# First pass of a fused attention and router block: transposing the normalised rows by 16 small transfers and VectorE instead of by TensorE

## The chip, the cores and the metric

The kernel runs on one core of a Trainium2 chip. The metric is the device time of one launch in microseconds (us), the median of several runs. Engines are named PE (TensorE matmul), PEld (its weight load), DVE (VectorE), ACT (ScalarE), POOL (GpSimd) and SP (SyncE, which issues every DMA here).

## What is computed

The input is 8192 rows of 512 numbers. A row is normalised, modulated, sent through a linear attention of 16 heads (sums over all rows come first, then each row is used again), added back, normalised again and sent through a router with eight small experts. The reference, cut to what matters here:

```python
h = _layernorm(x) * (1 + ca) + sa
q = elu(h @ Wq.T + bq) + 1 ;  k = elu(h @ Wk.T + bk) + 1 ;  v = h @ Wv.T + bv     # 16 heads of 32
KV = einsum('bhsd,bhsm->bhmd', k, v)
Z = 1 / (einsum('bhsd,bhd->bhs', q, k.sum(axis=2)) + 1e-6)
x = x + ga * (einsum('bshd,bhmd,bhs->bshm', q, KV, Z) @ Wo.T + bo)
h = _layernorm(x) * (1 + cb) + sb
x = x + gb * ffn(h)            # value projection, router with top 2 of 8, experts of 32 hidden units
```

## The kernel before

The rows are worked in 64 tiles of 128 rows. The **first pass** (to about 627 us) needs, for each tile, the normalised rows `xn` and their transpose `xT`; the second pass works in pairs of tiles and is not touched. Every engine runs its own list of instructions and the lists meet only at semaphores. Each engine has a function `step(i, s)`, called for i = -2 or -1 to 64; tile 20 to tile 59 are in a hardware loop of two steps a turn (`sweep`, `LOOP_A`), the rest is written out.

Products are taken at high precision by splitting each operand into a high part and a rest (`_hi`, `_lo`) and adding three products (function `three`, lines 1394, 1395 and 1399). One tile in step i goes as follows.

- PE: four 128x128 transposes of `xn(i+1)` into one PSUM bank, `bank_xT` (L1507); `k(i)` = 12 matmuls of `xT(i)` with `wk`; the sum M over rows of `k(i-1)` with `xn(i-1)`, 12 matmuls; `q(i)`, 12 matmuls with `wq`.
- ACT: the high part of `xT(i+1)` (L720), relu and exp for `q(i-1)` (L724, L726) and `k(i)` (L731, L733), the high parts of `k` (L737) and `xn` (L742).
- DVE: `zq(i-1)` (L1107), `xT_lo(i+1)` (L888), statistics of tile i+2 (L867), `qf(i-1)` (L1116), `zk(i)` (L1123), `xn(i+2)` (L882, after POOL has the reciprocal root, L593), `kf(i)` (L1132), `k_lo(i)` (L1138), then the next step's `zq`.
- SP: the load of tile i+4 (L538), special loads of step i (`loads`), the store of `q(i-1)` to DRAM (L543).

Steps 0 to 19 also carry the preparation of all weights, in a table `PREP` that gives each step up to three jobs; they put extra instructions on PE, ACT and DVE (for instance `modulation`, L990 and L993, and for six jobs `scaled`, L1014, which stands between `kf` and `k_lo`). The `loads` of step 2 fetch `Wo` in 16 transfers of short pieces (L500, `raw_o`).

Of the kernel before, what the change touches and what calls it, by code (L numbers as in the profile page):

```python
# [48 lines left out]
PREP = {0: ["", "", "bk", "bq"], 3: ["v0", "v1"], 4: ["v2", "v3"], 5: ["bv", ""], 6: ["", "ga"], 7: ["o0", "o1"],  # L49
# [17 lines left out]
def sweep(eng, step, first, last, loop_from, loop_to):  # L67

    for i in range(first, loop_from):
        step(i, i % 2)  # L70
    with eng.Fori(loop_from, loop_to, 2) as v:
        step(v, 0)
        step(v + 1, 1)
    for i in range(loop_to + 1, last + 1):
        step(i, i % 2)
# [28 lines left out]

def build(nc, x, Wq, bq, Wk, bk, Wv, bv, Wo, bo, fWv, fbv, Wg, bg, Wp, alpha, g_r, b_r, g_c, b_c,
# [3 lines left out]
    LOOP_A = (PREP_STEPS, T - 5)  # L109
# [9 lines left out]
    with ctx:  # L119
# [21 lines left out]
        ca1_col = sb("ca1_col", [P, KB])  # L141
        ks_acc = sb("ks_acc", [P, D])
# [171 lines left out]
        xT_psum = sem("xT_psum")  # L314
# [16 lines left out]
        q_out = [sem("q_out0"), sem("q_out1")]  # L331

# [123 lines left out]
        def _(sp):  # L456
# [88 lines left out]
            sweep(sp, step, -2, T, *LOOP_A)  # L545

# [22 lines left out]
        def _(pool):  # L569
# [35 lines left out]
            sweep(pool, step, -2, T - 1, *LOOP_A)  # L605
# [64 lines left out]
        def _(act):  # L670
# [36 lines left out]

            act.wait_ge(prep_taken, TAKE["sa"] + 1)
            for b in range(KB):
                hi_scaled(f"k{b}", wk_hi[:, b, :], ca1_col[:, b:b + 1])  # L710
            for b in range(KB):
                hi_scaled(f"q{b}", wq_hi[:, b, :], ca1_col[:, b:b + 1])


            def step(i, s):
                if live(i + 1, T):
                    act.wait_ge(xT_psum, i + 2)
                    wait_count(act, xTl_done, i)
                    wait_count(act, q_psum, i)
                    nc.scalar.copy(xT_hi[:, 1 - s, :], bank_xT).then_inc(xTh_done, 1)  # L720
# [7 lines left out]
                if live(i, T):  # L728
# [4 lines left out]
                    nc.scalar.activation(exp_k[:, s, :], exp_k[:, s, :], ACT.Exp, scale=-1.0).then_inc(ek_done, 1)  # L733
                    act.wait_ge(kf_done, i + 1)
# [10 lines left out]
            sweep(act, step, -1, T, *LOOP_A)  # L745
# [105 lines left out]
        def _(dve):  # L851
# [25 lines left out]
            def normed(i, s):  # L877
                dve.wait_ge(rstd_done, i + 1)
                wait_count(dve, xT_psum, i - 1)
# [3 lines left out]
                                        ALU.subtract, ALU.mult).then_inc(xn_done, 1)  # L883

# [48 lines left out]
            nc.vector.tensor_copy(sa_col[:], bank("sa")[:, 0:KB])  # L933
            taken_by(nc.vector.tensor_scalar(ca1_col[:], bank("sa")[:, KB:2 * KB], 1.0, None, ALU.add), "sa")
# [89 lines left out]
            def prepare(i, n):  # L1024

                for j in prep_job(i, n):
# [76 lines left out]
            def step(i, s):  # L1103
# [4 lines left out]
                if live(i + 1, T):  # L1108
                    xT_low(i + 1, 1 - s)
# [10 lines left out]
                if live(i, T):  # L1120
                    dve.wait_ge(k_psum, i + 1)
                    wait_count(dve, ek_done, i - 1)
                    nc.vector.tensor_tensor(zk[:, s, :], bank_k, bk_row[:], ALU.add).then_inc(zk_done, 1)  # L1123
                prepare(i, 0)
                if ahead:
                    var_eps(i + 2, s)
                    normed(i + 2, s)
                if live(i, T):
                    dve.wait_ge(ek_done, i + 1)
                    wait_count(dve, kh_done, i - 1)  # L1130
                    wait_count(dve, ks_done, i - 1)
# [17 lines left out]
            sweep(dve, step, 0, T, *LOOP_A)  # L1149
# [236 lines left out]
        def _(pe):  # L1386
# [23 lines left out]

            def blocks_of(raw, fb):
# [264 lines left out]
```

## Time and profile before

| | |
|---|---|
| median of 3 runs | 1314.85 us (1313.02 to 1316.6) |
| profiled execution | 1313.38 us, its span 1311.7 us |
| busy share of the span | PE 96%, PEld 79%, DVE 74%, ACT 41%, POOL 43% |
| mean granted TensorE clock | 0.991 |
| `zq` of tile 0, of tile 19, and of tile 63 on DVE | 38.1 us, 243.4 us, 626.8 us |

The span is from the first to the last instruction; the 1.7 us beside it lie outside. A matmul's end is modelled, so how far apart the starts of two matmuls lie says more than their durations.

### The profile page before, as it was taken

Reading aid. Unit: us, or ns where it says so; the run is one execution under the profiler, and the core shown is the slowest. Engines: PE = TensorE matmul, PEld = TensorE weight load, DVE = VectorE, ACT = ScalarE, POOL = GpSimd, SP = SyncE. Lnnn points to the kernel's source line nnn. Section 1 sums busy time; section 2 is a strip of 40 time slices with the busy share of each in tenths; the row PEclk is TensorE's granted clock in tenths of the full one; section 3 lists DMA queues with packets and bytes.
Section 4 is the critical chain, followed back from the end, with each engine's and each line's share of the span. In section 5 each row is a group of like instructions: output and inputs, shape, how many; then the busy total and the mean of one; then the engine's idle time right before and its main releaser. Section 6 shows DMA issues by size and latency. Waiting matters only on the chain.

```text
span 1311.7 us, 19601 instructions
## 1 busy us (share of the span) xinstructions
PE 1255.9 (96%) x6078; PEld 1034.4 (79%) x6078; DVE 973.8 (74%) x2195; ACT 541.7 (41%) x1125; POOL 557.9 (43%) x397
## 2 busy tenths in 40 slices
PE   7999999999999999999779999999999999999998
PEld 7777877788888888888568888878888888888887
DVE  7778887866666666665767778777778788787764
ACT  2443544454444444444234344343343343433431
POOL 1332333344344334433346455455464454554631
PEclk8999999999999999999899999999999999999999
DMA  6643211111122111111312231231321322312201
GB/s 208 161 150 88 65 49 49 49 64 64 48 63 64 61 51 64 64 51 47 104 49 77 69 97 60 86 97 49 98 82 63 97 67 79 97 57 89 81 17 49
DMA packets 93467, 99.12 MB, mean 76 GB/s; under 512 B 21720, under 2 KB 54616, under 8 KB 93392
## 3 DMA queue, kind: packets, MB, share of 16 engines
q1 hardware_dynamic: 93392, 98.21, 24.1%
q8 instruction: 37, 0.61, 0.2%
q14 instruction: 38, 0.31, 0.1%
HBM read 64.63 MB, written 33.55 MB: 75 GB/s over the span
## 4 chain that ended last, share of the span: by engine, by line
PE 56%; POOL 15%; issue 13%; DVE 7%; ACT 2%; DMA 0%; POOLq 0%; SPq 0%; ACTq 0%; DVEq 0%
PE ps L1395 17%; PE ps L1394 17%; PE ps L1399 17%; POOL xb L610 6%; POOL rrs L649 3%; PE ps L1593 2%; POOL xn_lo L602 2%; POOL rstd L642 2%; DVE x L1222 2%; DVE xT_lo L1229 1%; PE ps L1507 1%; POOL ks_acc L598 1%; DVE marked L1312 1%; ACT xn L806 1%; POOL rstd L593 1%
## 5 line engine op out<-in xcount | busy, mean ns | idle before, releaser
L636 POOL TENSOR_TENSOR cn<-c,half 128x16 f32<-128x16 f32 x32 | 104.2, 3255 | 281.5 <-DVE c L1257 281.5
L593 POOL TENSOR_TENSOR rstd<-veps,neg_half 128x1 f32<-128x1 f32 x64 | 35.2, 550 | 286.3 <-DVE veps L875 286.3
L598 POOL TENSOR_TENSOR ks_acc<-ks_acc,kf 128x512 f32<-128x512 f32 x64 | 82.9, 1295 | 102.7 <-DVE kf L1132 102.7
L602 POOL TENSOR_TENSOR xn_lo<-xn,xn_hi 128x512 fp32r<-128x512 f32 x64 | 110.9, 1733 | 7.4 <-ACT xn_hi L742 7.4
L1394 PE MATMUL ps<-g_hi,qT_hi 128*128 128x512 f32 x256 | 104.6, 409 | 4.9 <-ACT qT_hi L770 4.9
L1138 DVE TENSOR_TENSOR k_lo<-kf,k_hi 128x512 fp32r<-128x512 f32 x64 | 75.4, 1178 | 43.8 <-ACT k_hi L737 36.5
L1394 PE MATMUL ps<-wk_hi,xT_hi 128*128 128x512 f32 x256 | 106.2, 415 | 0.0
L1394 PE MATMUL ps<-k_hi,xn_hi 128*128 128x512 f32 x256 | 102.7, 401 | 1.4 <-DVE bq_row L1051 1.4
L1394 PE MATMUL ps<-wq_hi,xT_hi 128*128 128x512 f32 x256 | 103.7, 405 | 0.0
L1394 PE MATMUL ps<-v_hi,xT_hi 128*128 128x512 f32 x256 | 102.6, 401 | 0.0
L1395 PE MATMUL ps<-g_lo,qT_hi 128*128 128x512 f32 x256 | 101.9, 398 | 0.0
L1395 PE MATMUL ps<-wq_lo,xT_hi 128*128 128x512 f32 x256 | 101.3, 396 | 0.0
L1395 PE MATMUL ps<-wk_lo,xT_hi 128*128 128x512 f32 x256 | 101.3, 396 | 0.0
L1399 PE MATMUL ps<-k_hi,xn_lo 128*128 128x512 f32 x256 | 101.2, 395 | 0.0
L1395 PE MATMUL ps<-k_lo,xn_hi 128*128 128x512 f32 x256 | 101.1, 395 | 0.0
L1395 PE MATMUL ps<-v_lo,xT_hi 128*128 128x512 f32 x256 | 100.0, 391 | 0.0
L763 ACT CAST xT_hi<-ps 128x512 fp32r<-128x512 f32 x64 | 37.5, 587 | 132.3 <-PE ps L1593 132.3
L731 ACT ACTIVATE exp_k<-zk 128x512 f32<-128x512 f32 x64 | 40.4, 632 | 110.7 <-DVE zk L1123 110.7
L628 POOL TENSOR_TENSOR qks<-q_in,ks_q 128x1024 f32<-128x1024 f32 x32 | 77.1, 2409 | 14.9 <-DMA q_in<-q_scratch 8.3
L1394 PE MATMUL ps<-c_hi,xT_hi 128*128 128x328 f32 x256 | 80.7, 324 | 0.0
L610 POOL TENSOR_TENSOR xb<-xin,bo_ga 128x1024 f32<-128x1024 f32 x32 | 78.3, 2446 | 1.7 <-PE ps L1399 1.6
L720 ACT CAST xT_hi<-ps 128x512 fp32r<-128x512 f32 x64 | 37.5, 586 | 98.6 <-PE ps L1507 98.6
(241 smaller groups left out, 3358.3 us busy)
## 6 DMA issues: line engine op xcount, KB each, us to landing
xin<-_attn_hidden_states_dram SPq DMA_DIRECT2D x64, 256.0 KB, 2.8
q_scratch<-qf SPq DMA_DIRECT2D x64, 256.0 KB, 2.9
xin<-_attn_hidden_states_dram SPq DMA_DIRECT2D x32, 512.0 KB, 4.1
q_in<-q_scratch SPq DMA_DIRECT2D x128, 128.0 KB, 2.9
out_dram<-qf SPq DMA_DIRECT2D x64, 256.0 KB, 2.1
wm_in<-in_L_wmod_dram SPq DMA_DIRECT2D x4, 1024.0 KB, 6.9
wm_in<-in_L_wmod_dram SPq DMA_DIRECT2D x4, 512.0 KB, 6.7
raw_k<-in_L_attn_Wk_dram SPq DMA_DIRECT2D x1, 1024.0 KB, 10.1
```

The costliest lines, as they stand in the source:

```text
L593: nc.gpsimd.tensor_tensor(rstd[:, s:s + 1], veps[:, s:s + 1], neg_half[:, 0:1], ALU.pow).then_inc(rstd_done, 1)
L598: nc.gpsimd.tensor_tensor(ks_acc[:], ks_acc[:], kf[:, s, :], ALU.add).then_inc(ks_done, 1)
L602: nc.gpsimd.tensor_tensor(xn_lo[:, 1 - s, :], xn[:, 1 - s, :], f32(xn_hi[:, 1 - s, :]), ALU.subtract).then_inc(xnl_done, 1)
L610: nc.gpsimd.tensor_tensor(xb[:], xin[:], bo_ga[:].unsqueeze(1).to_broadcast([P, 2, D]), ALU.add).then_inc(xb_done, 1)
L628: nc.gpsimd.tensor_tensor(qks[:].rearrange("p h (g f) -> p (h g) f", f=P), q_of(j).rearrange("p (n f) -> p n f", f=P), ks_q[:].unsqueeze(1 ...
L636: nc.gpsimd.tensor_tensor(cn[:].rearrange("p h e -> p (h e)"), c2[:].rearrange("p h e -> p (h e)"), half[:], ALU.pow).then_inc(cn_done, 1)
L649: nc.gpsimd.tensor_tensor(rrs[:].rearrange("p h k -> p (h k)"), rve[:], neg_half[:, 0:4], ALU.pow).then_inc(rrs_done, 1)
L731: nc.scalar.activation(exp_k[:, s, :], zk[:, s, :], ACT.Relu, scale=-1.0).then_inc(rk_done, 1)
L1138: nc.vector.tensor_tensor(k_lo[:, s, :], kf[:, s, :], f32(k_hi[:, s, :]), ALU.subtract).then_inc(kl_done, 1)
L1394: nc.tensor.matmul(dst, ah, bh, start=start and n == 0, stop=False)
L1395: nc.tensor.matmul(dst, ah, bl, start=False, stop=False)
L1399: last = nc.tensor.matmul(dst, al_, bh, start=False, stop=stop and n == len(parts) - 1)
```

## The change

`xn` of a tile is no longer transposed on PE (apart from tiles 0 and 1). Instead SP issues 16 SBUF-to-SBUF transfers, each 32 partitions by 128 numbers, which move the blocks of `xn` into a new buffer `xq`; DVE then transposes `xq` in blocks of 32x32 straight into `bank_xT` (`turned_x`). To make that possible the blocks of `xT` hold every fourth column instead of 128 neighbours, so `wk` and `wq` and their scales are prepared for that order (`every_fourth`, `sa4_col`, `ca4_col`), and the scales in the old order are made by a new preparation job `sc` in step 1. The read of `xq` steps over four numbers for each one that it takes (`f` is outside `j` in memory).

On ACT the high part of `xT` moves from the start of the step to between exp and `k_hi`; on DVE `xT_lo` moves from behind `zq` to between `kf` and `k_lo`. `kf` is now written over `zk`. On SP the step's special loads come last. All first-pass steps are written out; the hardware loop is gone. The diff, cut:

```diff
-PREP = {0: ["", "", "bk", "bq"], 3: ["v0", "v1"], 4: ["v2", "v3"], 5: ["bv", ""], 6: ["", "ga"], 7: ["o0", "o1"],
+PREP = {0: ["", "", "bk", "bq"], 1: ["sc"], 3: ["v0", "v1"], 4: ["v2", "v3"], 5: ["bv", ""], 6: ["", "ga"], 7: ["o0", "o1"],
...
+def sweep_tiles(step, first, last):
+
+    for i in range(first, last + 1):
         step(i, i % 2)
...
+        xq = sb("xq", [P, 2, D], F32, early)
         exp_k = sb("exp_k", [P, 2, D], F32, early)
-        kf = sb("kf", [P, 2, D], F32, early)
+        kf = zk
...
             def step(i, s):
+                if live(i + 2, T) and i >= 0:
+                    sp.wait_ge(xn_done, i + 3)
+                    sp.wait_ge(xTb_done, i + 1)
+                    for g in range(KB):
+                        for c4 in range(KB):
+                            sp.dma_start(xq[DH * c4:DH * (c4 + 1), s, g * P:(g + 1) * P],
+                                         xn[DH * g:DH * (g + 1), s, c4 * P:(c4 + 1) * P]).then_inc(xq_in[s], 16)
                 if live(i + 4, T):
...
+            def turned_x(i, s):
+                dve.wait_ge(xq_in[s], regrouped(i, s))
+                dve.wait_ge(xTl_done, i)
+                nc.vector.transpose(bank_xT.rearrange("p (j g t) -> p g j t", j=KB, g=KB),
+                                    xq[:, s, :].rearrange("p (g f j) -> p g j f", g=KB, j=KB)).then_inc(xTb_done, 1)
...
+            def every_fourth(raw, fb):
+                return [raw[:, r, fb::KB] for r in range(KB)]
...
             pe.wait_ge(wk_in, 16)
             for b in range(KB):
-                transposes(f"k{b}", blocks_of(raw_k, b))
+                transposes(f"k{b}", every_fourth(raw_k, b))
...
             def step(i, s):
-                if live(i + 1, T):
+                if isinstance(i, int) and i <= 0:
                     pe.wait_ge(xn_done, i + 2)
...
                     for b in range(KB):
-                        blk = slice(b * P, (b + 1) * P)
-                        last = nc.tensor.transpose(bank_xT[:, blk], xn[:, 1 - s, blk], ident[:])
-                    last.then_inc(xT_psum, 1)
+                        last = nc.tensor.transpose(bank_xT[:, b * P:(b + 1) * P], xn[:, 1 - s, b::KB], ident[:])
+                    last.then_inc(xTb_done, 1)
```

DVE's list in step 2, before the change, from `zq` to the `k_lo` of the same step:

```order
L1107 TENSOR_TENSOR zq<-ps,bq_row 128x512 [waits eq_done,q_psum]
L888 TENSOR_TENSOR xT_lo<-ps,xT_hi 128x512 [waits q_psum,xTh_done]
L867 BN_STATS stats<-xin 128x6 [waits x_in0]
L1116 SCALAR_TENSOR_TENSOR qf<-zq,exp_q 128x512 [waits eq_done,stats_done]
L871 BN_AGGR mv<-stats 128x2
L1123 TENSOR_TENSOR zk<-ps,bk_row 128x512 [waits ek_done,k_psum]
L875 TENSOR_SCALAR veps<-mv 128x1 [waits mv_done]
L882 TENSOR_SCALAR xn<-xin,mv,rstd 128x512 [waits xnh_done,xnl_done,xT_psum,rstd_done]
L1132 SCALAR_TENSOR_TENSOR kf<-zk,exp_k 128x512 [waits ks_done,kh_done,ek_done]
L1138 TENSOR_TENSOR k_lo<-kf,k_hi 128x512 [waits m_done,kh_done,kf_done]
```

The same step after the change (`kf` bears the name `zk`, over which it is written):

```order
L1134 TENSOR_TENSOR zq<-ps,bq_row 128x512 [waits q_psum]
L882 BN_STATS stats<-xin 128x6 [waits x_in0]
L1144 SCALAR_TENSOR_TENSOR qf<-zq,exp_q 128x512 [waits eq_done,stats_done]
L886 BN_AGGR mv<-stats 128x2
L1152 TENSOR_TENSOR zk<-ps,bk_row 128x512 [waits ks_done,kh_done,k_psum]
L890 TENSOR_SCALAR veps<-mv 128x1 [waits mv_done]
L900 TENSOR_SCALAR xn<-xin,mv,rstd 128x512 [waits xnh_done,xnl_done,xq_in0,rstd_done]
L906 STREAM_TRANSPOSE ps<-xq 128x4x4x32 [waits xTl_done,xq_in1]
L1161 SCALAR_TENSOR_TENSOR zk<-zk,exp_k 128x512 [waits ek_done]
L912 TENSOR_TENSOR xT_lo<-ps,xT_hi 128x512 [waits q_psum,xTh_done]
L1169 TENSOR_TENSOR k_lo<-zk,k_hi 128x512 [waits m_done,kh_done,kf_done]
```

One 128x512 transpose is new, behind `xn`, and waits for the 16 transfers of the tile before (`xq_in1`); `xT_lo` stands between `kf` and `k_lo`.

SP's list from step 1's special loads to step 2's, before:

```order
L495 DMA bv_row<-in_L_attn_bv_dram 128x4x32 x4
L543 DMA q_scratch<-qf 128x512 [waits qf_done]
L538 DMA xin<-in_L_attn_hidden_states_dram 128x512 [waits xn_done]
L500 DMA raw_o<-in_L_attn_Wo_dram 128x4x32 x16
L543 DMA q_scratch<-qf 128x512 [waits qf_done]
```

And after, down to the transfers of step 3:

```order
L498 DMA bv_row<-in_L_attn_bv_dram 128x4x32 x4
L544 DMA xq<-xn 32x128 [waits xTb_done,xn_done]
L544 DMA xq<-xn 32x128 x15
L548 DMA xin<-in_L_attn_hidden_states_dram 128x512 [waits xn_done]
L551 DMA q_scratch<-qf 128x512 [waits qf_done]
L503 DMA raw_o<-in_L_attn_Wo_dram 128x4x32 x16
L544 DMA xq<-xn 32x128 [waits xTb_done,xn_done]
L544 DMA xq<-xn 32x128 x15
```

Each step's 16 transfers now stand behind the special loads of the step before, in one queue.

## Rows read from the trace of the kernel before

**Rows 1.** Windows: us, busy of each engine (instructions), clock, DMA share, GB/s.

```profile
150.00:250.00 100.00, 96.89 (x442) 76.54 (x441) 82.73 (x145) 44.50 (x78) 32.65 (x28) 1.00 0.16 49
262.00:590.00 328.00, 328.00 (x1491) 266.18 (x1491) 220.67 (x375) 155.87 (x263) 132.24 (x113) 1.00 0.19 59
```

**Rows 2.** Timeline of PE: start us, duration us, what, idle before.

```profile
407.27 0.48 PE L1394 MATMUL ps<-wk_hi,xT_hi 128*128 128x512 f32 x1
...
416.07 0.48 PE L1394 MATMUL ps<-wk_hi,xT_hi 128*128 128x512 f32 x1
...
618.27 0.39 PE L1394 MATMUL ps<-wk_hi,xT_hi 128*128 128x512 f32 x1
...
626.63 0.40 PE L1394 MATMUL ps<-k_hi,xn_hi 128*128 128x512 f32 x1
```

**Rows 3.** Timeline of DVE in the loop.

```profile
407.11 0.69 DVE L1107 TENSOR_TENSOR zq<-ps,bq_row 128x512 f32<-128x512 f32 x1 [0.74 <-PE ps L1399]
```

**Rows 4.** Timeline of DVE, the ends of the preparation and its waits.

```profile
38.11 0.69 DVE L1107 TENSOR_TENSOR zq<-ps,bq_row 128x512 f32<-128x512 f32 x1
...
89.59 0.69 DVE L1107 TENSOR_TENSOR zq<-ps,bq_row 128x512 f32<-128x512 f32 x1 [1.56 <-PE ps L1399]
...
196.41 0.69 DVE L1107 TENSOR_TENSOR zq<-ps,bq_row 128x512 f32<-128x512 f32 x1 [1.10 <-PE ps L1399]
...
202.52 0.56 DVE L943 SCALAR_TENSOR_TENSOR c_lo<-ps,cb_col,c_hi 128x328 fp32r<-128x328 f32 x1 [2.18 <-ACT c_hi L677]
...
243.37 0.69 DVE L1107 TENSOR_TENSOR zq<-ps,bq_row 128x512 f32<-128x512 f32 x1
```

**Rows 5.** Timeline of DVE, one written-out step (step 18).

```profile
220.58 0.69 DVE L1107 TENSOR_TENSOR zq<-ps,bq_row 128x512 f32<-128x512 f32 x1
...
222.69 0.69 DVE L1116 SCALAR_TENSOR_TENSOR qf<-zq,exp_q 128x512 f32<-128x512 f32 x1 [0.22 <-DVE stats L867]
...
223.39 0.66 DVE L1123 TENSOR_TENSOR zk<-ps,bk_row 128x512 f32<-128x512 f32 x1
...
224.77 0.55 DVE L882 TENSOR_SCALAR xn<-xin,mv,rstd 128x512 f32<-128x512 f32 x1 [0.66 <-POOL rstd L593]
225.41 0.69 DVE L1132 SCALAR_TENSOR_TENSOR kf<-zk,exp_k 128x512 f32<-128x512 f32 x1
226.84 1.18 DVE L1138 TENSOR_TENSOR k_lo<-kf,k_hi 128x512 fp32r<-128x512 f32 x1 [0.74 <-ACT k_hi L737]
227.95 0.68 DVE L1075 TENSOR_TENSOR b2raw<-ps,b2raw 128x512 f32<-128x512 f32 x1
```

**Rows 6.** Groups of DVE instructions, each shape apart: busy us, mean ns | idle before.

```profile
L1239 DVE STREAM_TRANSPOSE qTf<-qz 128x1024 f32<-128x1024 f32 x32 | 39.6, 1238 | 0.1
...
L1211 DVE TENSOR_TENSOR qz<-q_in,zr 128x1024 f32<-128x1024 f32 x32 | 39.2, 1226 | 1.1
...
L1020 DVE TENSOR_TENSOR v_lo<-wtmp,v_hi 128x512 fp32r<-128x512 f32 x4 | 7.1, 1776 | 0.0
```

**Rows 7.** Timeline of DVE, a step with `scaled` (step 12).

```profile
161.25 0.75 DVE L1014 SCALAR_TENSOR_TENSOR wtmp<-ps,cb_col,mod 128x512 f32<-128x512 f32 x1
162.07 1.18 DVE L1138 TENSOR_TENSOR k_lo<-kf,k_hi 128x512 fp32r<-128x512 f32 x1
```

**Rows 8.** Timeline of SP's DMA issues: start us, time to issue all.

```profile
45.02 5.01 SPq L495 DMA_DIRECT2D bv_row<-in_L_attn_bv_dram  x4
...
52.95 10.65 SPq L500 DMA_DIRECT2D raw_o<-in_L_attn_Wo_dram  x16
...
123.76 1.99 SPq L520 DMA_DIRECT2D b2raw<-in_L_ffn_b_dram  x6
...
645.65 1.79 SPq L531 DMA_DIRECT2D q_in<-q_scratch  x4
```

**Rows 9.** DMA issues: KB each, median us from issue to landing.

```profile
out_dram<-qf SPq DMA_DIRECT2D x64, 256.0 KB, 2.1
```

**Rows 10.** Timeline of PEld, the first weight transposes.

```profile
15.03 3.46 PEld L1407 LDWEIGHTS ps<-ident,raw_k 128*128 128x128 f32 x16
```

More of the change, by code:

```diff
@@ L64, in wait_count @@
         eng.wait_ge(sem, n)
[L67 to L74, printed above, removed]
+def sweep_tiles(step, first, last):
+    for i in range(first, last + 1):
         step(i, i % 2)
@@ L543, in step @@
                     sp.dma_start(q_dram[rows(i - 1), :], qf[:, 1 - s, :]).then_inc(q_out[1 - s], 16)
-            sweep(sp, step, -2, T, *LOOP_A)
+                if isinstance(i, int):
+                    loads(i)
+            sweep_tiles(step, -2, T)
             sp.wait_ge(q_out[0], landed(T - 2, 0))
@@ L733, in step @@
                     nc.scalar.activation(exp_k[:, s, :], exp_k[:, s, :], ACT.Exp, scale=-1.0).then_inc(ek_done, 1)
+                    if live(i + 1, T) and i > 0:
+                        xT_high(i, s)
                     act.wait_ge(kf_done, i + 1)
@@ L743, in step @@
                 prepare(i, 1)
-            sweep(act, step, -1, T, *LOOP_A)
+            sweep_tiles(step, -1, T)
             act.wait_ge(m_done, T)
@@ L878, in normed @@
                 dve.wait_ge(rstd_done, i + 1)
-                wait_count(dve, xT_psum, i - 1)
+                if isinstance(i, int) and i <= 3:
+                    wait_count(dve, xTb_done, i - 1)
+                else:
+                    dve.wait_ge(xq_in[s], regrouped(i - 2, s))
                 wait_count(dve, xnh_done, i - 1)
@@ L1127, in step @@
                     normed(i + 2, s)
+                if live(i + 1, T) and not early_turn:
+                    turned_x(i + 1, 1 - s)
                 if live(i, T):
                     dve.wait_ge(ek_done, i + 1)
-                    wait_count(dve, kh_done, i - 1)
-                    wait_count(dve, ks_done, i - 1)
                     nc.vector.scalar_tensor_tensor(out=kf[:, s, :], in0=zk[:, s, :], scalar=0.0,
@@ L1134, in step @@
                     scaled(i)
+                    if live(i + 1, T) and not early_turn:
+                        xT_low(i + 1, 1 - s)
                     dve.wait_ge(kf_done, i + 1)
@@ L1147, in step @@
                     router_constants()
-            sweep(dve, step, 0, T, *LOOP_A)
+            sweep_tiles(step, 0, T)
             dve.wait_ge(m_done, T)
@@ L1433, in _, with strided_columns @@
             all_rows, first_row = ones[:, 0:1], ident[:, 0:1]
+            def strided_columns(j, col, part):
+                for b in range(KB):
+                    last = nc.tensor.matmul(bank(j)[:, col + b:col + b + 1], part[:, b::KB], all_rows, start=True, stop=True)
+                return last
             pe.wait_ge(mod1_done, KB)
-            columns("sa", 0, [(mod1[:, 0, :], all_rows)])
-            columns("sa", KB, [(mod1[:, 1, :], all_rows)]).then_inc(prep_psum, 1)
+            strided_columns("sa", 0, mod1[:, 0, :])
+            strided_columns("sa", KB, mod1[:, 1, :]).then_inc(prep_psum, 1)
             pe.wait_ge(wk_in, 16)
             for b in range(KB):
-                transposes(f"k{b}", blocks_of(raw_k, b))
+                transposes(f"k{b}", every_fourth(raw_k, b))
             pe.wait_ge(wq_in, 16)
             for b in range(KB):
-                transposes(f"q{b}", blocks_of(raw_q, b))
+                transposes(f"q{b}", every_fourth(raw_q, b))
             SUMS = {"ga": 0, "gb": 3}
@@ L1454, in prepare @@
                         sum_rows(j, acc_q[:])
+                    elif j == "sc":
+                        bank_free(pe, j)
+                        columns(j, 0, [(mod1[:, 0, :], all_rows)])
+                        columns(j, KB, [(mod1[:, 1, :], all_rows)]).then_inc(prep_psum, 1)
                     elif j in SUMS:
@@ L1540, in step @@
                 prepare(i, 2)
-            sweep(pe, step, -1, T, *LOOP_A)
+            sweep_tiles(step, -1, T)
             pe.wait_ge(ks_done, T)
```

51 lines of the change are left out of this document (30 added, 21 removed).

## The prediction

> **What bounds the kernel now.** I read the windows first. In the loop (262 to 590 us) PE is busy in all of 328 us, and DVE in 221; in the preparation DVE's share is higher, 83 of 100 us [rows 1]. So the first pass has two regimes, and I asked of each which wait ends last.
>
> In the loop it is PE. One tile takes 416.07 - 407.27 = 8.80 us, and DVE's first instruction of the step waits 0.74 us for PE's last matmul [rows 2, 3]. The trace also holds one tile without the four transposes, at the end of the pass: from 618.27 to 626.63 PE does the same 36 matmuls in 8.36 us, 0.232 each [rows 2]. The transposes therefore cost **0.44 us a tile**: their own time and the slower first matmul behind them (0.48 against 0.39 us).
>
> In the preparation it is DVE. Its `zq` starts at 38.11 us for tile 0 and at 243.37 for tile 19: 19 steps of 10.8 us on average, and in all of them only three waits that come from PE, 1.56 and 1.10 us directly and 2.18 through ACT [rows 4]. What PE saves in these steps is worth nearly nothing, and what DVE gets in addition is paid in full, unless it falls into a hole of DVE's own.
>
> **PE's part.** From step 22 on, after two steps in which DVE catches up, to step 62 there are 41 steps: 41 x 0.44 = **-18.0 us**. In the two stretches of the preparation that PE sets (ended by the waits of 1.56 and of 1.10 with 2.18) it saves one transposition each, **-0.9**.
>
> **DVE's step.** The written-out step 18 gives its length without PE [rows 5]: `zq` to `qf` 2.11, set by relu and exp on ACT, since DVE idles 0.22 ahead of `qf`; `qf` to `zk` 0.70; `zk` to `xn` 1.38, with 0.66 of waiting for POOL; `xn` 0.47; `kf` to `k_lo` 1.43, with 0.74 of waiting for ACT's `k_hi`; `k_lo` 1.11. Sum 7.20. (An instruction frees DVE some 0.08 before its listed end: `k_lo` is listed with 1.18 and the next starts after 1.11.) `xT_lo`, 0.61, leaves a place where ACT sets the pace and goes into the 0.74 hole: nothing gained and nothing lost. Its cover is gone in six steps, where `scaled` fills that hole already: there `k_lo` starts 0.82 after a `scaled` of 0.75 [rows 7], room for 0.15 to 0.18, so 0.43 each, **+2.6**. ACT's copy of the high part runs beside `kf`, ahead of `k_hi`, and is no longer than `kf`.
>
> **The new transpose.** The nearest row is `turned_q`: 1.24 us for 1024 numbers a partition, the same as a plain two-input operation of that size, 1.23 [rows 6]. At that rate 512 numbers take 0.69 (like `qf` in rows 5), which occupies 0.61. But `turned_q` reads runs of 32 neighbours, while `turned_x` reads one number in four, each 16 bytes from the last. No row here shows such a read. I bound it by 0.69 below and by the whole 1.24 above, twice the time for a number, and take the upper end, **1.24, occupying 1.16**, because nothing of the neighbour that a read brings along can be used. The slowest 512-number row of DVE, 1.78 [rows 6], bounds it for the rival.
>
> The Trainium skill (Vector Engine (DVE) Microarchitecture Reference, Measured stream behaviour on trn2) speaks against the change here: a port keeps its full rate only while it reads at least two adjacent 4-byte words at a time; a source that hops every element took 1.73 ns a column against 1.05, and 2.5 with small steps. By those figures an estimate for this transpose is 1.0 to 1.4 us, and my sum would be 5 us lower or 9 higher.
>
> The transpose stands in steps 1 to 19 of the preparation. In two of them the waits for PE absorb it, so 17 x 1.16 = **+19.7 us**. In the later steps DVE's step becomes 7.20 + 1.16 = 8.36, exactly PE's 8.36. Two engines with no room between them lose a little; I take 8.40, 41 x 0.04 = **+1.6**.
>
> **The transfers.** SP's 16 issues follow the end of `xn(i+2)`; the transpose of that tile follows the end of `xn(i+3)`, one step later. Issue: six short transfers took 1.99 us, 0.33 each, four of 128 KB 1.79, 0.45 each [rows 8]. A transfer of 32 short rows is nearer to the former: 16 x 0.34 = 5.4. Landing: 2.1 us is the shortest of the large ones [rows 9]. With 0.2 for SP to notice, the transpose can start 0.2 + 5.4 + 2.1 = 7.7 us after `xn`, and a step has 8.4: hidden, with 0.7 to spare. If they are late by more, the order lets DVE run on in between: two steps must hold one DVE step and one transfer time X, so the step is (8.36 + X)/2 and nothing is lost up to X = 8.4. SP itself needs 5.4 + 0.7 for the load and the store, of 8.4. The load of tile i+4 and the store are now 5.4 later, but are needed more than a step later.
>
> In the preparation the special loads are ahead of the next transfers in the queue. Steps 1 and 2 are the heavy ones. A step there is 10.8 + 1.0 = 11.8 long with the new transpose. Step 1: 5.4 + 0.9 + 5.0 for `bv_row` [rows 8] + about 1.7 for three large loads = 13.0: 1.2 late. Step 2: 5.4 + 0.7 + 10.65 of `raw_o` [rows 8] = 16.8, and step 3's transfers need 7.5 more: 1.2 + 24.3 against two steps of 11.8, a stall of **+1.9** in step 4. Behind it stand `kf`, `k_lo` and so PE's M. Nothing at all or 8 us, if the pieces of `raw_o` drain slowly, are the ends. The other loads fit.
>
> **Small parts.** Job `sc`: two short DVE operations and a wait, **+0.5**; its eight PE columns lie where PE waits for DVE. The 32 weight transposes read every fourth column; 16 weight loads took 3.46 us [rows 10], between nothing and double for these, mostly beside DVE's work, **+1.0**. The loop's disappearance: the written-out steps show the same 0.232 between matmuls; nothing.
>
> **Sum.** -18.0 - 0.9 + 2.6 + 19.7 + 1.6 + 1.9 + 0.5 + 1.0 = **+8.4 us** on the profiled execution's 1313.4, 1321.8. The median of the runs shown lies 1.5 higher, within their spread; I predict 1322. A measurement here tells a difference of about 0.3% (3.9 us) from none.
>
> **Rivals.**
> 1. *The strided read costs nothing extra* (0.69). For it: the transpose reshuffles anyway and `turned_q` shows no price over a plain operation [rows 6]; against it the stride above. 17 x 0.61 = 10.4 in place of 19.7, and no 1.6: -2.5, 1311. This is the side that isn't slower. The balance is at a duration of 0.84 us. If the stall and the start-up term also fail to appear it is -5.4, 1308. Chance 0.26.
> 2. *The transfers are late in every step.* If 16 issues take 0.45 each, as for `q_in`, X = 7.2 + 2.1 + 0.2 = 9.5 and the step (8.36 + 9.5)/2 = 8.93: 41 x 0.53 = 22 more, 1344. At `raw_o`'s 0.67 each SP alone needs 11.3 a step, and the pass would be 120 us longer. Against it: the pieces are few and long compared with those. Chance 0.13.
> 3. *DVE becomes the bound*: a transpose over 1.24. At 1.43 the step is 8.55: 3.2 more in the preparation and 41 x 0.15 = 6.2, 1331; at 1.78 it is 1352. By the Trainium skill's figure for small steps (same page and section) this is the case that comes. Chance 0.15.
> 4. Something in the start-up or the catching up that I don't see, either way: 0.04.
>
> The forecast has 0.42; alone it spans 1315 to 1329. **Range** 1309 to 1340: it leaves out rival 1 with both favours, and the far ends of 2 and 3. Faster by over 0.3%: 0.10 from rival 1, 0.03 from the forecast's edge, 0.03 others, **0.16**. Within 0.3%: 0.14 and 0.08, **0.22**. Slower: **0.62**.
>
> **What would show it.** In the profile after: the transpose's mean duration (0.69 or 1.24); the distance between PE's `wk_hi` groups in the later tiles (8.36 to 8.40; 8.5 or more would be DVE or the transfers, told apart by whether DVE waits for `xq` ahead of the transpose); DVE's `zq` of tile 19 at some 243.4 + 25 = 268 us, and no wait for PE left there beyond two; one wait for `xq` of about 2 us near 80 us; SP's issue time of 16 transfers, 5.4; the second pass of unchanged length. I am wrong if the transpose is cheap, if transfers issue at over 0.4 us each, or if DVE's holes, into which I put `xT_lo`, close.

## The result, and the profile after

The changed kernel takes **1480.86 us** (median, 1479.95 to 1484.14) against 1315.32 (1313.02 to 1316.6) before: 1.1275 times as long, interval 1.1256 to 1.1295. The forecast was 1322, range 1309 to 1340.

The page of the changed kernel: busy time of PE and DVE, the clock, the chain that ended last, and three groups and an issue row.

```profile
PE 1288.9 (87%) x5846; PEld 1041.6 (70%) x5846; DVE 1025.2 (69%) x2259; ACT 545.7 (37%) x1125; POOL 558.2 (38%) x397
...
PEclk9969899989999999999999899999999999999999
...
SPq 31%; PE 24%; issue 20%; POOL 14%; DVE 7%; ACT 2%; DMA 1%; POOLq 0%; ACTq 0%; DVEq 0%
SPq L544 28%; PE ps L1425 7%; PE ps L1426 7%; PE ps L1430 7%; POOL xb L620 5%; POOL rrs L659 3%; POOL xn_lo L612 2%; PE ps L1636 2%; POOL ks_acc L608 2%; SPq L548 2%; POOL rstd L652 1%; DVE x L1253 1%; DVE xT_lo L1260 1%; SPq L551 1%; POOL rstd L603 1%
...
L1425 PE MATMUL ps<-wk_hi,xT_hi 128*128 128x512 f32 x256 | 123.3, 481 | 135.7 <-ACT xT_hi L722 133.7
...
L906 DVE STREAM_TRANSPOSE ps<-xq 128x512 f32<-128x512 f32 x62 | 67.9, 1096 | 170.7 <-DMA xq<-xn 170.6
...
xq<-xn SPq DMA_DIRECT2D x992, 16.0 KB, 1.8
```

The chain is where to begin: 28% of the span hangs on SP's queue at L544, the line that issues the new transfers. Not on DMA (1%), whose transfers land 1.8 us after their issue, and not on DVE. DVE waited 170.6 us for `xq`, PE 133.7 us for ACT's `xT_hi`, which stands behind DVE's transpose: the same stall, seen one and two engines further on.

The windows of [rows 1], after the change:

```profile
150.00:250.00 100.00, 82.64 (x343) 63.46 (x342) 75.51 (x128) 37.61 (x65) 27.79 (x23) 0.93 0.27 71
262.00:590.00 328.00, 266.77 (x1044) 205.79 (x1042) 201.96 (x337) 121.98 (x203) 99.81 (x85) 0.94 0.25 69
```

PE does 1044 matmuls in 328 us, where it did 1491 (four of 40 a tile being transposes). No compute engine is full any more. Which one is shows in the timeline of SP (start us, time to issue all):

```profile
497.69 10.02 SPq L544 DMA_DIRECT2D xq<-xn  x16
507.76 0.58 SPq L548 DMA_DIRECT2D xin<-_attn_hidden_states_dram  x1
508.38 0.43 SPq L551 DMA_DIRECT2D q_scratch<-qf  x1
508.91 10.40 SPq L544 DMA_DIRECT2D xq<-xn  x16
519.36 0.58 SPq L548 DMA_DIRECT2D xin<-_attn_hidden_states_dram  x1
519.98 0.43 SPq L551 DMA_DIRECT2D q_scratch<-qf  x1
520.51 10.02 SPq L544 DMA_DIRECT2D xq<-xn  x16
```

SP has no gap: 16 issues, the load, the store, the next 16. A round is 11.22 and then 11.60 us, and 0.63 to 0.65 us of it goes to each of the 16. Over all tiles behind the 20th a round averages 11.5 us; in about half of the rounds the 16 issues take longer than 10.0, up to 11.2, and the trace doesn't say why. The pass runs at SP's pace. DVE's timeline in the same place, the ends of one step:

```profile
501.25 0.68 DVE L1134 TENSOR_TENSOR zq<-ps,bq_row 128x512 f32<-128x512 f32 x1
...
505.56 0.55 DVE L900 TENSOR_SCALAR xn<-xin,mv,rstd 128x512 f32<-128x512 f32 x1 [0.66 <-POOL rstd L603]
508.94 1.09 DVE L906 STREAM_TRANSPOSE ps<-xq 128x512 f32<-128x512 f32 x1 [2.83 <-DMA xq<-xn]
...
510.69 0.69 DVE L912 TENSOR_TENSOR xT_lo<-ps,xT_hi 128x512 fp32r<-128x512 f32 x1
511.36 1.18 DVE L1169 TENSOR_TENSOR k_lo<-zk,k_hi 128x512 fp32r<-128x512 f32 x1
512.46 0.68 DVE L1134 TENSOR_TENSOR zq<-ps,bq_row 128x512 f32<-128x512 f32 x1
```

The wait for `xq` (2.83 us) is the only long one; `k_lo` follows `xT_lo`, and `zq` follows `k_lo`, without a hole. The row names DMA, since the last landing releases it; but the last issue of that tile only ended at 507.7 (first row of SP above), 1.2 us before DVE starts. The issue was late, not the landing.

Three rows of DVE split the time: `zq` of tiles 0, 19 and 63, as in [rows 4] and, for the last, 626.83 in the kernel before.

```profile
38.08 0.69 DVE L1134 TENSOR_TENSOR zq<-ps,bq_row 128x512 f32<-128x512 f32 x1
...
297.21 0.69 DVE L1134 TENSOR_TENSOR zq<-ps,bq_row 128x512 f32<-128x512 f32 x1
...
794.41 0.68 DVE L1134 TENSOR_TENSOR zq<-ps,bq_row 128x512 f32<-128x512 f32 x1
```

The same differences for every kernel of this study, in us, read off these rows of each. They are used throughout below; the last column is the span less the `zq` of tile 63, which is the end of the first pass and the whole second.

| kernel | first `zq` | tile 0 to 19 | tile 19 to 63 | rest of the span |
|---|---|---|---|---|
| before | 38.11 | 205.26 | 383.46 | 684.87 |
| after | 38.08 | 259.13 | 497.20 | 687.69 |
| no_transfers | 39.43 | 221.87 | 366.48 | 685.72 |
| no_transfers_contig | 39.69 | 213.56 | 366.11 | 687.64 |
| eight_wide | 38.19 | 225.48 | 366.49 | 685.84 |
| from_dram | 38.17 | 234.52 | 386.20 | 686.01 |
| two_queues | 38.02 | 237.54 | 367.35 | 687.19 |
| bounce | 39.34 | 221.63 | 366.49 | 684.84 |
| bounce_late | 38.79 | 206.01 | 366.48 | 684.72 |

Of the 170.4 us that the span grew, 53.9 lie in the preparation, 113.7 in the tiles behind it, 2.8 after. The start is as it was. The 113.7 are a mean over unlike tiles: 497.20 / 44 is 11.30, less than a round of SP, since the last tiles have no transfers to wait for (tile 62 to 63 takes 7.24).

### The profile page after: what moved, and what is told of

Same layout as the page of the kernel before. It is cut to its first block, busy times and chain, and to the rows that moved or that the text cites. A ratio compares the mean times of both kernels' runs of the same rounds, so it can differ in the third digit from the quotient of the medians.

```text
span 1482.1 us, 19445 instructions
## 1 busy us (share of the span) xinstructions
PE 1288.9 (87%) x5846; PEld 1041.6 (70%) x5846; DVE 1025.2 (69%) x2259; ACT 545.7 (37%) x1125; POOL 558.2 (38%) x397
## 4 chain that ended last, share of the span: by engine, by line
SPq 31%; PE 24%; issue 20%; POOL 14%; DVE 7%; ACT 2%; DMA 1%; POOLq 0%; ACTq 0%; DVEq 0%
SPq L544 28%; PE ps L1425 7%; PE ps L1426 7%; PE ps L1430 7%; POOL xb L620 5%; POOL rrs L659 3%; POOL xn_lo L612 2%; PE ps L1636 2%; POOL ks_acc L608 2%; SPq L548 2%; POOL rstd L652 1%; DVE x L1253 1%; DVE xT_lo L1260 1%; SPq L551 1%; POOL rstd L603 1%
## 5 line engine op out<-in xcount | busy, mean ns | idle before, releaser
L1425 PE MATMUL ps<-wk_hi,xT_hi 128*128 128x512 f32 x256 | 123.3, 481 | 135.7 <-ACT xT_hi L722 133.7
L608 POOL TENSOR_TENSOR ks_acc<-ks_acc,zk 128x512 f32<-128x512 f32 x64 | 82.7, 1293 | 324.7 <-DVE zk L1161 324.7
L906 DVE STREAM_TRANSPOSE ps<-xq 128x512 f32<-128x512 f32 x62 | 67.9, 1096 | 170.7 <-DMA xq<-xn 170.6
L1425 PEld LDWEIGHTS ps<-wk_hi,xT_hi 128*128 128x128 f32 x256 | 56.3, 220 | 171.9 <-ACT xT_hi L722 157.9
L1426 PE MATMUL ps<-wk_lo,xT_hi 128*128 128x512 f32 x256 | 117.5, 459 | 0.0
L737 ACT ACTIVATE exp_q<-zq 128x512 f32<-128x512 f32 x64 | 40.4, 632 | 135.5 <-DVE zq L1134 135.5
L1144 DVE SCALAR_TENSOR_TENSOR qf<-zq,exp_q 128x512 f32<-128x512 f32 x64 | 44.3, 693 | 54.0 <-DVE stats L882 48.3
```

The costliest lines, as they stand in the source:

```text
L608: nc.gpsimd.tensor_tensor(ks_acc[:], ks_acc[:], kf[:, s, :], ALU.add).then_inc(ks_done, 1)
L906: nc.vector.transpose(bank_xT.rearrange("p (j g t) -> p g j t", j=KB, g=KB), xq[:, s, :].rearrange("p (g f j) -> p g j f", g=KB, j=KB)).th ...
L1144: nc.vector.scalar_tensor_tensor(out=qf[:, 1 - s, :], in0=zq[:, 1 - s, :], scalar=0.0, in1=exp_q[:, 1 - s, :], op0=ALU.max, op1=ALU.add).t ...
L1425: nc.tensor.matmul(dst, ah, bh, start=start and n == 0, stop=False)
L1426: nc.tensor.matmul(dst, ah, bl, start=False, stop=False)
```

## The experiments

The theory: one engine's time for issuing is the bound, because an SBUF-to-SBUF transfer costs SyncE about 0.6 us to issue whatever its size, and there are sixteen a tile. The rivals: the landing or the DMA engines are too slow; the turn on VectorE, the stride or the written-out steps cost the time; the price goes by bytes or by rows.

**probe_issues.** The price by itself, after the kernel before has ended. One of the groups, the others alike:

```diff
             sp.wait_ge(stored[1], landed(T - 1, 1))
+            for g in range(KB):
+                for c4 in range(KB):
+                    sp.dma_start(xin[DH * c4:DH * (c4 + 1), 0, g * P:(g + 1) * P],
+                                 xn[DH * g:DH * (g + 1), 0, c4 * P:(c4 + 1) * P]).then_inc(probe, 16)
+            done[0] += 16
+            sp.wait_ge(probe, 16 * done[0])
```

> The kernel before, with transfers added behind its last store, in groups that SyncE issues one after the other, each group waited for before the next; each group has a line of its own. They overwrite no output. Groups: 16 of the change's shape (32 partitions by 128 elements, SBUF to SBUF, across partitions), 16 of it within the same partitions, 16 from DRAM, 16 to DRAM, 16 of 8 partitions by 128, 16 of 8 by 512, 16 of one row of 128, 8 of 128 by 128 SBUF to SBUF, 8 of 128 by 128 from DRAM, 8 of 32 by 256, 2 whole tiles in, 2 out, and 4 of the change's shape alone, each waited for. Theory 'SBUF at both ends': the first two groups cost SyncE 0.60 to 0.65 us a transfer with nothing else running, those with DRAM at one end 0.33 to 0.45. Rival 'rows': the price follows the partitions of the transfer, so 8 partitions and one row cost clearly less than 32 (0.35 against 0.65) and 128 more. Rival 'any transfer': all cost 0.6 or more, one row too. Rival 'full queue': the four single ones cost 0.35 and only long rows of issues 0.65.

Timeline of SP behind the last store. In this order: the change's shape, the same within partitions, from DRAM, to DRAM, 8 partitions by 128, 8 by 512, one row, 128 by 128 in SBUF, the same from DRAM, 32 by 256, and the single ones (in their row the time holds three of the waits).

```profile
1314.95 10.12 SPq L570 DMA_DIRECT2D xin<-xn  x16
1326.29 10.00 SPq L575 DMA_DIRECT2D xin<-xn  x16
1337.52 7.32 SPq L580 DMA_DIRECT2D xin<-q_scratch  x16
1346.05 7.28 SPq L585 DMA_DIRECT2D q_scratch<-xn  x16
1354.42 11.11 SPq L589 DMA_DIRECT2D xin<-xn  x16
1366.64 10.63 SPq L593 DMA_DIRECT2D xin<-xn  x16
1378.64 10.04 SPq L597 DMA_DIRECT2D xin<-xn  x16
1389.82 5.07 SPq L601 DMA_DIRECT2D xin<-xn  x8
1396.25 3.70 SPq L605 DMA_DIRECT2D xin<-q_scratch  x8
1401.43 5.00 SPq L610 DMA_DIRECT2D xin<-xn  x8
...
1413.80 5.72 SPq L622 DMA_DIRECT2D xin<-xn  x4
```

With SBUF at both ends a transfer costs 0.63 us from issue to issue (10.12 / 16), with DRAM at either end 0.46 (7.32 / 16). Bytes and rows hardly matter among these shapes, all of which move pieces of 512 bytes or more: one row of 128 elements 0.63, 128 by 128 elements 0.63, 8 by 128 even 0.69. Short pieces are another case, which the probe leaves out: `raw_o` (512 pieces of 128 bytes each) comes from DRAM and costs 0.67, `bv_row` 1.25 [rows 8]. The trace's own duration of one is 0.591 us for the change's shape, 0.421 from DRAM, and 0.510 for the single ones, each waited for. So a little, 0.08 of 0.59, comes from issuing in a row; most is there with nothing ahead. "SBUF at both ends" holds, with the other kind just above the upper end of what I had put (0.45). "Rows", "any transfer" and "full queue" fall. What inside the issue takes the 0.17 more isn't visible in a trace.

**no_transfers.** Is that all, or does something else in the change cost time?

```diff
-                    sp.wait_ge(xTb_done, i + 1)
-                    for g in range(KB):
-                        for c4 in range(KB):
-                            sp.dma_start(xq[DH * c4:DH * (c4 + 1), s, g * P:(g + 1) * P],
-                                         xn[DH * g:DH * (g + 1), s, c4 * P:(c4 + 1) * P]).then_inc(xq_in[s], 16)
...
+            link(nc.vector.memset(xq[:], 0.0))
...
-                dve.wait_ge(xq_in[s], regrouped(i, s))
```

(SP's wait `xTb_done` and the wait for the transfers in `normed` go too. DVE now transposes zeros.)

> The changed kernel without its sixteen transfers a tile; VectorE transposes a buffer that was set to zero once, so the first pass works on zeros there (the output is not the reference's). Everything else of the change stays: the turn on VectorE, the strided weights, the written-out steps. Theory 'SyncE's issues bound the first pass': all of the 166 us goes with them and the time is 1300 to 1325 us, near the sum of the forecast's other terms (1322). Rival 'the turn itself or the written-out code costs': 1400 or more stays. Rival 'VectorE's access to every fourth element slows its neighbours': 1340 to 1380.

1314.34 us (1312.3 to 1318.94), ratio to before 1.0003, interval 0.9992 to 1.0015. All of the loss goes with the transfers. The long window:

```profile
262.00:590.00 328.00, 327.18 (x1409) 263.96 (x1408) 262.78 (x434) 167.48 (x276) 138.91 (x118) 1.00 0.21 63
```

PE is full again and the clock at its full 2.4 GHz. The table has what the change does without its transfers: +16.6 us in the preparation, -17.0 behind it. The steady tile takes 8.367 us (mean of the 20 from tile 40 to 60), as forecast from the one tile without transposes [rows 2]. The two signs cancel, and the rivals on the turn, the stride's effect on neighbours and the written-out code fall.

**eight_wide.** Price by the transfer or by the byte?

```diff
-                        for c4 in range(KB):
-                            sp.dma_start(xq[DH * c4:DH * (c4 + 1), s, g * P:(g + 1) * P],
-                                         xn[DH * g:DH * (g + 1), s, c4 * P:(c4 + 1) * P]).then_inc(xq_in[s], 16)
+                        for h in range(2):
+                            sp.dma_start(xq[DH * (3 - g):DH * (4 - g), s, h * 2 * P:(h + 1) * 2 * P],
+                                         xn[DH * g:DH * (g + 1), s, h * 2 * P:(h + 1) * 2 * P]).then_inc(xq_in[s], 16)
```

> The changed kernel with 8 transfers of 32 partitions by 256 elements a tile in place of 16 of 32 by 128: the same bytes, the same rows to each transfer, half the number of transfers; the elements land in other places, so the output is not the reference's. Theory 'a price for each transfer': 8 x 0.65 + 1.2 = 6.4 us of SyncE in a step of 8.4, nothing late, 1310 to 1330 us. Rival 'by bytes': each costs 1.3, SyncE needs 11.6 again, 1480. Rival 'landing or engines of the queue': the last transfer's landing of 1.8 us sets VectorE's start whatever the number, and 1380 or more stays.

1317.85 us (1316.83 to 1319.69), ratio 1.003, interval 1.002 to 1.004. The same bytes in half the transfers lose nothing in the steady tiles: 366.49 us from tile 19 to 63, like no transfers at all. By the transfer, then, among transfers with pieces of 512 bytes or more. Its SP timeline:

```profile
450.89 4.95 SPq L544 DMA_DIRECT2D xq<-xn  x8
455.88 1.18 SPq L548 DMA_DIRECT2D xin<-_attn_hidden_states_dram  x1
457.11 0.43 SPq L551 DMA_DIRECT2D q_scratch<-qf  x1
459.25 4.95 SPq L544 DMA_DIRECT2D xq<-xn  x8
```

0.62 each and 1.7 us free in the round. What it loses is one wait in the preparation, 4.98 us, at the transpose behind `raw_o`'s sixteen issues (DVE's timeline):

```profile
81.63 1.09 DVE L906 STREAM_TRANSPOSE ps<-xq 128x512 f32<-128x512 f32 x1 [4.98 <-DMA xq<-xn]
```

**from_dram.** The same sixteen with the cheaper kind of source.

```diff
-                                         xn[DH * g:DH * (g + 1), s, c4 * P:(c4 + 1) * P]).then_inc(xq_in[s], 16)
+                                         xt[rows(i + 2), :][DH * g:DH * (g + 1), c4 * P:(c4 + 1) * P]).then_inc(xq_in[s], 16)
```

> The changed kernel with the same sixteen destinations a tile, 32 partitions by 128 elements, but read from the input in DRAM in place of the normalized tile in SBUF; the first pass so works on x not normalized (the output is not the reference's). Theory 'SBUF at both ends costs': an issue falls to 0.33 to 0.45 us as the loads with DRAM at one end, 16 x 0.4 + 1.2 = 7.6 us a step, 1310 to 1335 us. Rival 'a price for each transfer of this shape, wherever it comes from': 0.65 again and 1470 to 1485 us.

1348.01 us (1346.43 to 1349.93), ratio 1.0255, interval 1.0238 to 1.0272. The theory was right in direction and its upper end 13 us short. SP's timeline:

```profile
445.59 7.38 SPq L544 DMA_DIRECT2D xq<-_attn_hidden_states_dram  x16
453.02 0.42 SPq L548 DMA_DIRECT2D xin<-_attn_hidden_states_dram  x1
453.49 0.43 SPq L551 DMA_DIRECT2D q_scratch<-qf  x1
454.09 7.40 SPq L544 DMA_DIRECT2D xq<-_attn_hidden_states_dram  x16
```

At 0.46 a transfer a round of SP is 8.5 us, already more than PE's 8.37, and SP still has no gap: 0.1 to 0.2 us between the store and the next transfers, where eight_wide has 1.7. As in the changed kernel, some groups of 16 take longer, 7.3 to over 8 us, and a round averages 8.8. So SP's issuing alone nearly gives the tile. The prediction's formula for a late chain gives almost the same: 7.4 of issues, 1.7 of landing (this kernel's median) and 0.2 are 9.3, and (8.2 + 9.3) / 2 = 8.75; the table has 386.20 / 44 = 8.78. This run doesn't tell the two apart. My expectation had neither the formula nor a price above 0.45.

**two_queues.** If one engine's issue time is short, a second engine's should do.

```diff
-                    for g in range(KB):
-                        for c4 in range(KB):
+                    for n in range(10):
+                        g, c4 = n // KB, n % KB
...
+            def pair(n0, s):
+                for n in (n0, n0 + 1):
+                    g, c4 = n // KB, n % KB
+                    nc.scalar.dma_start(xq[DH * c4:DH * (c4 + 1), s, g * P:(g + 1) * P],
+                                        xn[DH * g:DH * (g + 1), s, c4 * P:(c4 + 1) * P]).then_inc(xq_in[s], 16)
```

(`pair(10, s)` ahead of `xT_high`, `pair(12, s)` behind `xn_hi`, `pair(14, 1 - s)` in the next step ahead of relu.)

> The changed kernel with the same sixteen SBUF-to-SBUF transfers a tile, ten issued by SyncE and six by ScalarE, two in each of the three gaps that ScalarE has in a step (0.99, 1.56 and 1.50 us in the kernel without transfers). The result is that of the reference. Theory 'what is short is one engine's issue time': at 0.65 each SyncE needs 10 x 0.65 + 1.2 = 7.7 us, the chain behind xn 6.5 + 1.8 + 0.2 = 8.5 us, and ScalarE's pairs of 1.3 us nearly fit their gaps; the later steps go from 11.3 back to 8.4 to 8.6 and the time to 1315 to 1330 us. Rival 'SBUF-to-SBUF transfers as such are slow, or the issues of two engines share one generator': the step stays at 10 us or more, 1400 and over. Rival 'ScalarE pays': its step is 4.3 + 6 x 0.65 = 8.2 with waits, exp and the high parts come late, 9 to 9.5 us a step, 1345 to 1370.

1331.51 us (1330.48 to 1335.35), ratio 1.0143, interval 1.0117 to 1.0168; the expectation ended at 1330. The steady tiles are whole again: 367.35 us, 0.9 above no transfers. The same sixteen transfers land in time when two engines issue them, so the DMA engines' work on them wasn't the limit, and the rival of a shared generator falls. A second engine brings a queue of its own, so this run alone doesn't part the engine's time from its queue's; the probe's single transfers, 0.51 us each with nothing ahead of them, speak for the engine's. ACT's timeline, its queue's issues (ACTq) among its instructions:

```profile
485.61 0.63 ACT L745 ACTIVATE exp_q<-exp_q 128x512 f32<-128x512 f32 x1
485.62 1.25 ACTq L721 DMA_DIRECT2D xq<-xn  x2
487.72 0.63 ACT L752 ACTIVATE exp_k<-zk 128x512 f32<-128x512 f32 x1 [1.48 <-DVE zk L1166]
```

This pair starts with the instruction ahead of it and is done when `zk` comes; `exp_k` doesn't wait for it. The Trainium skill (DMA: Bandwidth & Descriptors, Issuing engines are not separate DMA queues) says that transfers started by different engines share the same 16 DMA engines, and that a second engine saves only the time to initiate them, which is "usually small relative to the DMA itself". That the two share them no run here shows; the mean busy share of the 16 in the later tiles is 0.25 in the changed kernel and 0.34 here, far from full. The second part doesn't hold here: sixteen issues take 10 us and a landing 1.8. What remains over the kernel without transfers lies nearly all in the preparation (237.54 us against 221.87): DVE's waits for `xq` there add up to 14.8 us, in steps where SyncE's special loads stand in the same queue.

**bounce.** Fewer issues for the same regrouping: one store to DRAM and four gathering loads.

```diff
-                    sp.wait_ge(xTb_done, i + 1)
-                    for g in range(KB):
...
+                    sp.dma_start(x_dram[rows(i + 2), :], xn[:, s, :]).then_inc(x_out[s], 16)
...
+                if live(i + 2, T) and i >= 0:
+                    sp.wait_ge(xTb_done, i + 1)
+                    sp.wait_ge(x_out[s], landed(i, s))
+                    for c4 in range(KB):
+                        sp.dma_start(xq[DH * c4:DH * (c4 + 1), s, :].rearrange("p (g f) -> p g f", f=P),
+                                     x_dram[rows(i + 2), c4 * P:(c4 + 1) * P].rearrange("(g i) f -> i g f", i=DH)
+                                     ).then_inc(xq_in[s], 16)
```

> The changed kernel with the regrouping taken through DRAM: one store of the normalized tile, a wait for it on SyncE, then four loads that gather the rows, 5 issues with DRAM at one end in place of 16 with SBUF at both. The result is that of the reference. Theory 'the count times the price of an issue': 5 x 0.42 + 0.9 = 3 us of SyncE; the chain of store, landing, four issues and landing is 0.4 + 2.5 + 1.8 + 2.5 = 7.2 us, under the 8.4 of a step, so nothing waits and the time is that of the kernel without transfers, 1312 to 1322 us. Rival 'latency, not issue, is the trouble': two landings one behind the other are over 8.4 us and VectorE waits for them as before, 1340 or more. Rival 'SyncE, blocked in the wait for the store, holds up its other work in the preparation': a stall or two near 80 us, 1320 to 1330.

1315.77 us (1313.68 to 1316.6), ratio 1.0009, interval 1.0 to 1.0019: level with no transfers at all. SP's timeline:

```profile
439.81 0.34 SPq L543 DMA_DIRECT2D x_scratch<-xn  x1
440.19 0.43 SPq L546 DMA_DIRECT2D xin<-_attn_hidden_states_dram  x1
440.67 0.44 SPq L549 DMA_DIRECT2D q_scratch<-qf  x1
441.90 1.78 SPq L554 DMA_DIRECT2D xq<-x_scratch  x4
```

3 us of issuing a tile. The detour moves more: the DMA engines' busy share in the long window is 0.41, where it was 0.19 before the change [rows 1], and DVE never waits for `xq`. The loads start 2.1 us after the store and are issued at 443.7; with the 2.4 us of their landing the chain is 6.3 us, under a step. Two landings, one behind the other, cost nothing here, and neither does SP's wait in the preparation (221.63 us to tile 19, 221.87 without transfers).

**no_transfers_contig.** What is the stride worth?

```diff
-                                    xq[:, s, :].rearrange("p (g f j) -> p g j f", g=KB, j=KB)).then_inc(xTb_done, 1)
+                                    xq[:, s, :].rearrange("p (g j f) -> p g j f", g=KB, j=KB)).then_inc(xTb_done, 1)
```

> The kernel without transfers, and VectorE's transpose reads neighbouring elements in place of every fourth (it works on zeros, so the output is not the reference's). Theory 'the stride is what makes the transpose 1.10 us': 0.69 us each, 17 x 0.41 = 7 us less in the preparation, nothing in the steps that TensorE sets: 1304 to 1310 us. Rival 'the 32x32 transpose of 512 numbers takes 1.1 however it reads': 1.10 and no difference, 1312 to 1316.

1308.82 us (1307.07 to 1313.08), ratio 0.9959, interval 0.9943 to 0.9975. The transpose's group:

```profile
L896 DVE STREAM_TRANSPOSE ps<-xq 128x512 f32<-128x512 f32 x62 | 44.7, 721 | 0.0
```

0.72 us in place of 1.10: reading every fourth number, each of 4 bytes, in place of neighbours costs 0.38 us. It is paid only where VectorE sets the pace: 8.3 us less up to tile 19, 0.4 behind it.

**bounce_late.** The version that the two halves of the table ask for: TensorE turns tiles 0 to 19, VectorE the others.

```diff
-                early_turn = isinstance(i, int) and i <= 0
+                early_turn = isinstance(i, int) and i <= 18
```

(and the same bound in SP's, ACT's and PE's step and in `normed`.)

> As the kernel through DRAM, but with TensorE transposing tiles 0 to 19 as it does tiles 0 and 1 in the changed kernel, and VectorE those after. Theory 'the turn is paid in full where VectorE sets the pace and gives 0.43 us a tile where TensorE does': the 18 us lost up to tile 19 stay away and the 42 later steps go from 8.77 to 8.37, 17 us, less 1 to 2 for small parts: 1297 to 1303 us, faster than both kernels. Rival 'the preparation is long for another reason than the turn' (order of the steps, the wait of zk for the buffer it shares with kf): 1310 to 1318, no faster than before.

1301.04 us (1297.91 to 1302.01), ratio 0.9899, interval 0.9885 to 0.9913: **1.0% faster than before**. DVE's `zq` of tiles 19 and 63:

```profile
244.80 0.69 DVE L1139 TENSOR_TENSOR zq<-ps,bq_row 128x512 f32<-128x512 f32 x1
...
611.28 0.69 DVE L1139 TENSOR_TENSOR zq<-ps,bq_row 128x512 f32<-128x512 f32 x1 [0.90 <-PE ps L1435]
```

The preparation costs 0.75 us more than before and the later tiles 17.0 less. The preparation was long because of the turn on VectorE. This edit takes back with it the places of `xT_hi` and `xT_lo` that the turn had moved, so the two aren't told apart; `kf` written over `zk`, job `sc`, the strided weights and the written-out steps stay, and cost together no more than the 0.75.

## Why the prediction was wrong, by its steps

**The step that failed: the price of one issue.** The prediction put it so: "A transfer of 32 short rows is nearer to the former: 16 x 0.34 = 5.4." Measured in the later tiles: 10.0 to 11.2 us, 0.63 to 0.70 each. I ranked the rows of [rows 8] by the length and number of the pieces. The probe shows that for pieces of 512 bytes and more these hardly matter, and that the memory at the two ends does, which none of those rows could show: all of them have DRAM at one end. So 0.34 wasn't bounded by them. Even with DRAM at one end this shape costs 0.46, more than I took. The upper row, `raw_o` at 0.67, should have stood for the unknown kind with far more weight than the 120 us "At `raw_o`'s 0.67" got inside a rival of 0.13, and the range should have reached it.

**Rival 2 was the case, in its worse branch.** Its sum for the steady tiles was near: 11.3 us of SP a step, where SP's rounds average 11.5. (That the table's 497.20 / 44 is 11.30 to the digit is luck, see there.) It was near by luck of the price too: 0.67 belongs to short pieces from DRAM. Its 120 us are 41 x (11.3 - 8.4). Measured against the kernel without transfers: 130.7 us in 44 tiles, and 37.3 more in the preparation, which the rival left out; together 168.0 (and 2.0 behind it, 1.4 less ahead).

**The other terms**, measured without transfers:

- *PE's part*, -18.0 in 41 steps: -17.0 in 44. The tile went from 8.80 to 8.367, as forecast. From tile 21 on it is -18.3; the two tiles ahead of it, in which DVE catches up, take 1.3 us more, since DVE's step is longer.
- *DVE's step*, 7.20 + 1.16 = 8.36 and a loss of 1.6 between two equal engines: the step is 8.2 (in no_transfers `zq` of tiles 19 and 20 stand at 261.30 and 269.48), 7.20 plus the 1.01 that a transpose of 1.10 occupies. PE has 0.17 of room, and the 1.6 doesn't exist. The 7.20 had a slip: it counts 0.47 from `xn` to `kf`, where [rows 5] have 225.41 - 224.77 = 0.64. The measured 8.2 shows that the 0.17 between isn't paid once the transpose stands there.
- *The transpose*: forecast 1.24, measured 1.10 to 1.11 in all kernels that read every fourth number. Rival 1's 0.69 is about the contiguous read's time (0.72). The estimate by the Trainium skill (Vector Engine (DVE) Microarchitecture Reference, Measured stream behaviour on trn2), 1.0 to 1.4 us, agrees at its lower end.
- *The preparation*: -0.9 + 2.6 + 19.7 + 0.5 = 21.9; by the measured transpose 17 x 1.01 it would be 19.4; measured +16.6. Nearly all of the 2.8 between is the +2.6 for the steps with `scaled`, which doesn't exist. Set side by side, `zq` to `zq`, before and in no_transfers, those six steps grew by 0.6 to 1.3 us, 0.94 on average, no more than the transpose alone; with 0.43 in addition it would be 1.4. DVE's `k_lo` says where `xT_lo` went: in these six steps it is listed with 0.75 to 0.81 us and not with 1.18 [rows 7] (one of them below), so `scaled`, `xT_lo` and `k_lo` take together what `scaled` and `k_lo` took. In step 12 POOL's `ks_acc` ran beside `k_lo` for 0.63 us before and for 0.20 here; whether that is the reason no run shows.

```profile
175.98 0.75 DVE L1160 TENSOR_TENSOR k_lo<-zk,k_hi 128x512 fp32r<-128x512 f32 x1
```

- *The strided weight transposes*, +1.0: nothing. The first `zq` stands at 38.08 against 38.11. Across the kernels it lies between 38.0 and 39.7, without a pattern that I can name.
- *The stall behind `raw_o`*, +1.9: it came, larger. With eight transfers it is 4.98 us; with sixteen DVE waits 8.69 us already at the transpose before and 10.51 at this one, 19.2 of the 37.3 us:

```profile
75.41 1.09 DVE L906 STREAM_TRANSPOSE ps<-xq 128x512 f32<-128x512 f32 x1 [8.69 <-DMA xq<-xn]
...
97.78 1.09 DVE L906 STREAM_TRANSPOSE ps<-xq 128x512 f32<-128x512 f32 x1 [10.51 <-DMA xq<-xn]
```

- *Landing*: forecast 2.1, measured 1.8. Right, and not the trouble.
- *Loop and second pass*: unchanged within 3 us, as said.

With the issue at its real price and all else as forecast, the sum for the later tiles alone would have been about 120 us higher. With 0.34 it came to +8.4, where the kernel without transfers shows 0.3. The rest of the working was right to within 8 us in its sum, and an engine that I had costed in one sentence decided the result.

## What to carry to other kernels

Add up the issue time of the engine that starts the transfers, per step, as for any other engine, and measure the issue with the same memories at both ends. Where many small transfers regroup a tile, their number is the cost, so a detour through DRAM with five issues beats sixteen direct ones, if a step covers two landings, as it does here. And a move of work from one engine to another belongs only in the stages in which the first one is the bound: done there alone, with the detour through DRAM, it gave 1.0%; done everywhere, with the same detour, nothing that can be measured.

## What the runs showed of the hardware that I had not expected

- Issuing a transfer on SyncE cost 0.63 to 0.69 us with SBUF at both ends, from one row of 512 bytes to 64 KB, and 0.46 with DRAM at one, for 16 and for 64 KB in pieces of 512 bytes. With pieces of 128 bytes from DRAM it was 0.67 (`raw_o`) and 1.25 (`bv_row`). On ScalarE's queue one was listed with hardly more (median 0.607 us against 0.591 on SyncE's in the same run), and both queues issued at once.
- A tile that goes through DRAM and back (one store, 2.1 us to the next issue, 1.8 for four issues, 2.4 to the landing) is regrouped sooner than by sixteen direct transfers: 6.3 us against 10.0 to 11.2 of issues and 1.8 of landing.
- The 32x32 transpose of 512 elements a partition takes 0.72 us from neighbouring elements and 1.10 from every fourth.
- In the changed kernel's first pass PE, waiting a fifth of the time, had a mean granted clock of 0.94, and its `wk_hi` matmuls, with which a tile begins, averaged 0.481 us, against 0.415 before. SP set the pace there, so no loss from it shows; with the waits gone the clock was 1.00.
